# A table of places for every step, turns written as an integer, and eight centrings moved to TensorE, in a kernel of two transformer layers

## The reference, cut to what matters

```python
xn = _layernorm(x)                         # first block
x = x + _L0_attn_ref(xn, ...) + _L0_ffn_ref(xn, Wg, Wu, Wd)
#   _L0_attn_ref: linear attention (elu + 1), layer norm, gated FFN of 341, layer norm
#   _L0_ffn_ref:  sum over 8 experts of silu(x @ Wg) * (x @ Wu) @ Wd, FFN 512, all tokens
xn = _layernorm(x)                         # second block
x = x + _L1_attn_ref(xn, ...) + _L1_ffn_ref(xn, ...)

# _L1_attn_ref, four times over:
x = x + _attention(_layernorm(x, ln1w, ln1b), aw, ab, pw, pb)
h = _layernorm(x, ln2w, ln2b)
x = x + gelu(h @ fw + fb) @ mw + mb
# _attention: q, k, v = h @ aw + ab; each becomes a quaternion
#   [x, x - previous token, x rolled by one head, cos(x)]
# out = hamilton(hamilton(q, k), v) -> spectral filter -> first part -> @ pw + pb
# _L1_ffn_ref: each token goes to the 2 best of 8 experts, gated FFN of 512, weighted sum
```

## Time and profile before

| | |
|---|---|
| median of 3 runs | 1509.45 us (1508.14 to 1509.75) |
| span of the profiled execution | 1503.8 us, first to last instruction |
| what lies around the span, against the median | 5.6 us |
| PE busy | 1395.6 us, 93% |
| DVE busy | 1250.3 us, 83% |
| ACT busy | 1042.7 us, 69% |
| POOL busy | 360.9 us, 24% |
| mean TensorE clock granted | 0.981 of full |

### The profile page before, as it was taken

How to read it: one execution, slowest core, us unless ns; L and a number is a source line. 1 busy time by engine, 2 the same in 40 slices (tenths; PEclk the granted TensorE clock), 3 DMA queues, 4 the chain that set the end, 5 groups by cost and what they waited for, 6 DMA issues and landing times.

```text
span 1503.8 us, 20880 instructions
## 1 busy us (share of the span) xinstructions
PE 1395.6 (93%) x6198; PEld 990.6 (66%) x6198; DVE 1250.3 (83%) x1511; ACT 1042.7 (69%) x2411; POOL 360.9 (24%) x251
## 2 busy tenths in 40 slices
PE   6999999999899999899999899999889999999858
PEld 4677766666566666566665667656677677777636
DVE  3344467877999989999959897999999999999996
ACT  6455757676886777766877768777857787776652
POOL 0001203110221402011131411131543353344410
PEclk9999999999999999999999999999999999999989
DMA  7763445335544554533363335355555556555244
GB/s 270 261 255 139 157 146 185 118 114 168 167 135 148 179 164 135 206 117 111 109 216 113 99 107 168 121 155 174 162 184 167 158 176 198 162 174 160 86 112 155
DMA packets 111243, 238.02 MB, mean 158 GB/s; under 512 B 13207, under 2 KB 52844, under 8 KB 109644
## 3 DMA queue, kind: packets, MB, share of 16 engines
q1 hardware_dynamic: 106588, 227.31, 47.9%
q0 software_dynamic: 4544, 9.38, 1.8%
HBM read 185.59 MB, written 43.86 MB: 153 GB/s over the span
## 4 chain that ended last, share of the span: by engine, by line
PE 44%; issue 20%; DVE 16%; ACT 9%; POOL 8%; DMA 2%; SPq 0%; ACTq 0%; POOLq 0%; DVEq 0%
PE bank L1363 8%; PE bank L1351 7%; PE bank L1353 6%; PE bank L1352 6%; POOL RSTD L1025 4%; PE bank L1543 3%; DVE AM L1087 3%; POOL ytok L1040 3%; ACT ROWS L865 2%; PE bank L1458 2%; DVE SH L1217 2%; DVE TA L1083 2%; PE bank L1452 1%; ACT ROWS L878 1%; DVE TA L1092 1%
## 5 line engine op out<-in xcount | busy, mean ns | idle before, releaser
L1025 POOL TENSOR_TENSOR RSTD<-SS,power_half 128x4 f32<-128x4 f32 x96 | 158.8, 1654 | 816.7 <-ACT ROWS L865 816.5
L1363 PE MATMUL bank<-SH,WD 128*128 128x512 f32 x512 | 263.6, 596 | 0.8 <-DVE X L1233 0.8
L1351 PE MATMUL bank<-NH,GU 128*128 128x512 f32 x512 | 245.5, 479 | 2.0 <-DMA GU<-halves 1.0
L1217 DVE TENSOR_TENSOR SH<-SH,bank 128x512 f32<-128x512 f32 x256 | 172.4, 682 | 76.4 <-ACT SH L853 46.4
L1087 DVE TENSOR_TENSOR AM<-AM,TA 128x1024 f32<-128x1024 f32 x192 | 230.2, 1219 | 0.9
L1083 DVE TENSOR_TENSOR TA<-QKV 128x2048 f32<-128x2048 f32 x96 | 219.5, 2287 | 1.2
L1353 PE MATMUL bank<-NL,GU 128*128 128x512 f32 x512 | 203.0, 397 | 0.0
L1352 PE MATMUL bank<-NH,GU 128*128 128x512 f32 x512 | 202.6, 396 | 0.0
L853 ACT ACTIVATE SH<-bank 128x512 f32<-128x512 f32 x256 | 153.1, 605 | 59.6 <-PE bank L1353 57.5
L878 ACT ACTIVATE ROWS<-bank,RSTD 128x128 f32<-128x128 f32 x384 | 110.0, 374 | 56.2 <-POOL RSTD L1025 50.8
L1578 PE MATMUL bank<-XT,GU 128*128 128x256 f32 x624 | 147.5, 381 | 0.3 <-DVE SH L1335 0.3
(11 more groups left out here) (232 smaller groups left out, 2764.8 us busy)
## 6 DMA issues: line engine op xcount, KB each, us to landing
GU<-halves SPq DMA_DIRECT2D x112, 512.0 KB, 4.2
QKV<-QKV SPq DMA_DIRECT2D x32, 720.0 KB
GU<-in_w_gu SPq DMA_DIRECT2D x39, 512.0 KB, 3.6
xg<-in_c_fill SPq DMA_DIRECT2D x8, 2080.0 KB
WD<-in_w_d SPq DMA_DIRECT2D x128, 128.0 KB, 2.2
FC<-ready_w SPq DMA_DIRECT2D x32, 512.0 KB, 5.2
WQ<-ready_w SPq DMA_DIRECT2D x32, 384.0 KB, 4.8
WD<-in_w_d SPq DMA_DIRECT2D x39, 256.0 KB, 3.8
```

The costliest lines, as they stand in the source:

```text
L1025: pool.tensor_tensor(RSTD[:], SS[:], (power_one if k[0] == "at" else power_half)[:], ALU.pow).then_inc(power_done, 1)
L1217: dve.tensor_tensor(SH[:, g % 4, :], SH[:, g % 4, :], banks[2 + g % 2][:], ALU.mult).then_inc(h_ready, 1)
L1351: pe.matmul(out, w_hi, x_hi, start=True, stop=False)
L1363: pe.matmul(banks[4][:], WD1[:, slot, :], SH[:, g % 4, :], start=first, stop=last).then_inc(down_done, 1)
```

## The change

Three things are changed.

First, the turns of q, k and v are written once, as an integer: `turns` (ACT) writes x / 2 pi + 1/4 into an int32 view of `TURNS`, which rounds it; `reduce` (DVE) multiplies that integer by 2 pi and subtracts x; `cosines` takes Sin with a bias of plus or minus half pi. The step `round`, one ACT instruction of 1536 columns for each of the 32 layers, is gone. `turns` now waits for the earlier `cosines`, since it writes the buffer that these read.

Second, in four layers, (7, 3), (7, 2), (6, 3) and (5, 3), both scalings (A and C) are centred by PE, as in the first block: 8 scalings lose their DVE step, and ACT squares with a constant bias.

Third, the planner and its numbers are gone. `PLACES` has for each step and engine the place in that engine's list; `schedule()` only turns it into lists. As sets, the lists hold the same steps as before but for the 32 `round` and the 8 `centre` on DVE. No step of PE stands more than 13 of 969 places away from where it stood, none of DVE more than 25 of 1217.

```diff
-TURN = 6.283185
-class Plan:
...
+TURN = 2 * np.pi
+HALF_PI = 1.570796
+INSIDE = 1 - 2.5e-7
+CENTRED_BY_PE = ((7, 3), (7, 2), (6, 3), (5, 3))
+PLACES = {
+    "raw": {
+        "SP": (0, 1, 5, 8, 15, 21, 27, 30,),
+    },
...
+TAKES_PART = {
+    ("centre", "DVE"): lambda key: key[0] in ("A", "C") and key[1:3] not in CENTRED_BY_PE,
...
-    token_means = [x for x in scalings if x[0] in ("A", "C")]
+    token_means = [x for x in scalings if x[0] in ("A", "C") and x[1:3] not in CENTRED_BY_PE]
...
-    sums_before = count_before("ACT", ("keys_exp", "query"), lambda name, key: name == "scale" and key[0] == "at")
+    sums_before = count_before("DVE", ("keys_exp", "query"), lambda name, key: name == "normed" and key[0] == "at")
...
             elif name == "turns":
                 h = half_of[k]
                 act.wait_ge(view_read, upto("views", k + (2,)))
-                act.activation(own(QKV[:, h, :, 3, :]), own(QKV[:, h, :, 0, :]), ACT.Identity, bias=quarter[:],
+                act.wait_ge(cos_done, n)
+                act.activation(TURNS[:].bitcast(I32), own(QKV[:, h, :, 0, :]), ACT.Identity, bias=quarter[:],
                                scale=1.0 / (2 * np.pi)).then_inc(turns_done, 1)
-            elif name == "round":
-                h = half_of[k]
-                act.wait_ge(turns_done, upto("turns", k))
-                act.wait_ge(cos_done, n)
-                act.activation(TURNS[:], own(QKV[:, h, :, 3, :]), ACT.Identity, bias=rounder[:]).then_inc(rounded, 1)
             elif name == "cosines":
                 h = half_of[k]
                 act.wait_ge(reduced, upto("reduce", k))
-                act.activation(own(QKV[:, h, 0:2, 3, :]), TURNS[:, 0:2, :], ACT.Sin, scale=-TURN)
-                act.activation(own(QKV[:, h, 2, 3, :]), TURNS[:, 2, :], ACT.Sin, scale=TURN).then_inc(cos_done, 1)
+                act.activation(own(QKV[:, h, 0:2, 3, :]), TURNS[:, 0:2, :], ACT.Sin, bias=half_pi[:], scale=-INSIDE)
+                act.activation(own(QKV[:, h, 2, 3, :]), TURNS[:, 2, :], ACT.Sin, bias=minus_half_pi[:], scale=INSIDE).then_inc(cos_done, 1)
...
             elif name == "reduce":
                 h = half_of[k]
-                dve.wait_ge(rounded, upto("round", k))
-                dve.scalar_tensor_tensor(TURNS[:], TURNS[:], ROUND, own(QKV[:, h, :, 3, :]),
-                                         ALU.subtract, ALU.subtract).then_inc(reduced, 1)
+                dve.wait_ge(turns_done, upto("turns", k))
+                dve.scalar_tensor_tensor(TURNS[:], TURNS[:].bitcast(I32), TURN, own(QKV[:, h, :, 0, :]),
+                                         ALU.mult, ALU.subtract).then_inc(reduced, 1)
```

More of the change, by code:

```diff
@@ L10 @@
 BF16 = mybir.dt.bfloat16
+I32 = mybir.dt.int32
 ALU = mybir.AluOpType
@@ new lines, with step_keys @@
+TAKES_PART = {
+    ("centre", "DVE"): lambda key: key[0] in ("A", "C") and key[1:3] not in CENTRED_BY_PE,
+    ("centre", "ACT"): lambda key: key[0] != "at",
+    ("normed", "ACT"): lambda key: key[0] in ("n0", "n1", "n3", "A", "C"),
+    ("normed", "DVE"): lambda key: key[0] != "n3",
+    ("route", "ACT"): lambda key: key[1] in (0, 2),
+    ("route", "PE"): lambda key: key[1] == 2,
+    ("route", "DVE"): lambda key: key[1] != 2,
+}
+def step_keys():
+    lt = [(t, l) for t in range(TILES) for l in range(LAYERS)]
+    scalings = [(kind, t) for kind in ("n0", "at", "n1", "n2", "n3") for t in range(TILES)]
+    scalings += [(kind, t, l) for kind in ("A", "C") for t, l in lt]
+    tiles, blocks = list(range(TILES)), list(range(BLOCKS))
+    twice = [(g, i) for g in blocks for i in range(2)]
+    out = {name: list(range(n)) for name, n in (
+        ("raw", EXPERTS), ("split", EXPERTS), ("keep", EXPERTS), ("visit", TILES * SPAN // 2), ("split_attn", 1),
+        ("load_prep", LAYERS), ("prep", LAYERS), ("prep_centre", LAYERS), ("keep_prep", LAYERS), ("load_gain", 1),
+        ("last_down", 1), ("kv_sum", BATCHES), ("load_numbers", 1), ("table", 2))}
+    for name in ("fill", "add_experts", "keys", "keys_exp", "query", "ffn2_down", "ffn2_add", "save", "logits", "load_kept",
+                 "total", "load_y", "back", "merge", "out"):
+        out[name] = tiles
+    for name in ("load_w", "load_x", "turn_in", "down", "y_out"):
+        out[name] = blocks
+    for name in ("gate_up", "silu", "mult", "y_store"):
+        out[name] = twice
+    for name in ("load_q", "load_f", "load_p", "load_m", "roll", "turns", "differences", "reduce", "cosines", "fold", "freq",
+                 "gain", "proj", "proj_add", "fc_a", "fc_b", "mproj", "mlp_add"):
+        out[name] = lt
+    for name in ("centre", "power", "scale", "turn", "normed"):
+        out[name] = scalings
+    out["den"] = [(t,) for t in tiles]
+    out["expert"] = [(t, s) for t in tiles for s in range(SPAN)]
+    out["ffn2"] = [(t, c) for t in tiles for c in range(3)]
+    out["route"] = [(t, i) for t in tiles for i in range(4)]
+    out["scatter"] = [(t, i) for t in tiles for i in range(2 * GROUPS)]
+    out["views"] = [(t, l, j) for t, l in lt for j in range(VIEWS)]
+    out["ham"] = [(t, l, i) for t, l in lt for i in range(HAM + 2)]
+    return out
@@ L1050, in _ @@
         dve.memset(every_row[:], 1.0)
[L1051 removed]
+        dve.memset(half_pi[:], HALF_PI)
+        dve.memset(minus_half_pi[:], -HALF_PI)
         dve.memset(quarter[:], 0.25).then_inc(const_set, 1)
```

658 lines of the change are left out of this document (354 added, 304 removed), and 129 rows, old and new, of the table PLACES.

## The result

| | before | after |
|---|---|---|
| median | 1508.9 us (1508.14 to 1509.75, 4 runs) | 1483.97 us (1483.49 to 1484.69, 4 runs) |
| span of the profiled execution | 1503.8 us | 1482.2 us |
| mean clock granted | 0.981 | 0.990 |

The ratio is 0.9835, 95% interval 0.9821 to 0.9849. The forecast of 1485.4 us is 1.4 us off, and the range 1465 to 1503 holds the time. The sum behind it was less good than that: its total was near, its parts were not where it put them.

A forecast was written before the change was run, and what follows sets the result against it. PE was taken to lead from 200 to 1000 us and DVE from 1000 to 1477; 8.8 in the first, 6.1 + 9 in the second and 0.1 at the end make 24.0 us, 1509.45 to 1485.4 us, range 1465 to 1503.

The forecast's parts named there:

- The median against the span: Whole run: the sum was made against the 1503.8 us span, with the median kept 5.6 us above it.
- First stretch, 8.8 us: 200 to 1000 us, where PE leads: half of PE's 17.6 us of named waits saved by the new places; bounds 0 and 41.6.
- the very same neighbours: First stretch: four PE gaps (about 327, 503, 793, 850 us) whose neighbouring steps are unchanged, against five with more work ahead.
- SP and POOL: I count nothing: Weight loads and fills: they keep their distance to their users by a few steps, so 0 us was counted.
- Second stretch, 6.1 + 9 us: 1000 to 1477 us, where DVE leads: 6.1 us from seven centre steps off DVE, 9 us of its 21.2 us idle.
- The latency of a scaling: `turn` of layer (5, 3): some 3 us off PE's 5.13 us gap, 1.4 us of it seen by DVE.
- beside the other engines: ACT: 32 `round` steps, 51.5 us, leave an engine with slack; counted only through waits, not by itself.
- The integer operand: 32 `reduce` steps on DVE: reading int32 costs zero; the rival that it costs gave 1515 us, chance 0.07 with all else slower.
- the end: After the last `freq`, layer (7, 3): PE's queue decides and the new order gives 0.1 us.
- the counts: Signs in the profile: `round` absent, DVE's row sums 56 instead of 64, ACT busy near 994 us.
- The lists are not a new plan: All lists: each `freq` stands behind nearly the same expert work as before, with shifts of a few steps.

The follow-up runs named there:

- new_swap: Changed kernel with one DVE row sum back behind the first product of layer (4, 0) and `fill` 7 back ahead of its roll: 1490.8 us, 0.9891 of the kernel before.
- old_fill: Kernel before with one SP instruction moved, `fill` 7 behind the rolls of (4, 0) and (3, 2): 1503.9 us, 0.9979 of the kernel before.
- new_ctr2: Changed kernel with the eight centre steps back on DVE, three of them placed earlier than in a first try: 1490.4 us, 0.9885 of the kernel before.
- old_ctr: Kernel before, its own lists, with only the eight scalings centred by PE and their DVE steps dropped: 1508.9 us, 1.0005 of the kernel before.

## Why the prediction was right, and where it was not

- **The median against the span: 3.8 us, by luck on my side.** I carried 5.6 us between span and median. Each later profiled execution has a time of its own, and it is 1.8 us over its span in all of them (1484.02 for 1482.2 after). So the span that I worked from belonged to an execution some 3.8 us quicker than the median that I set it against, if the same holds for it. Against the span the forecast was 24.0 us and the gain 21.6; against the median it was 24.9. The sum was 2.4 us too hopeful (1479.8 against a span of 1482.2) and the distance 3.8 us too long, and what is left of the two is the 1.4 us.
- **First stretch, 8.8 us: too small, and for another reason.** It gave 14.5 us, and 15.9 if counted from the first `freq` behind 200 us, where the changed kernel was 1.4 us late. Half of 17.6 us of waits, 14.5 of them at `turn`, was to go; those at `turn` fell by 0.7 us only. For the same work, from that `freq` to the end of the first block's experts, PE's idle time fell by 7.7 us (40.5 to 32.8) and its busy time by 8.2 (748.0 to 739.8, at a clock of 0.99 and 1.00). So the size of the saved idle time was near and its place wrong, and the sum had no term for the clock in this stretch. Two thirds of the 14.5 us came from the part with the two stalls. Both, at 793 and 850 us, I had listed among the places with "the very same neighbours": I looked at PE's list alone, and the cause of the first stood in DVE's and SP's.
- **"SP and POOL: I count nothing": failed.** new_swap and old_fill show that `fill` 7 and one DVE step set 3 to 8 us. I had asked only who uses what the fill writes, and not which transfer was queued behind it: the roll behind it took 9.0 us instead of 5.1.
- **Second stretch, 6.1 + 9 us: too large, it gave 7.0 us** to the last `freq`. The 6.1 us of centring are real in the lists that were made for them (at most 7.1 us, new_ctr2) and nil in the old ones (old_ctr). Most of the 9 us from DVE's idle time did not come: DVE's wait for Silu fell by 4.1 us, that for XSH rose by 4.5. For the same work, from the end of the first block's experts to the last `freq` (447.4 us before, 440.5 after), DVE's busy time fell by 4.1 us (426.7 to 422.6) and its idle time by 2.8 (20.7 to 17.9). From 1000 us to 1455, just ahead of the last `freq`, DVE is busy 437.08 of 455 us, the 96% that I expected, so it does lead; it led before too.
- **The latency of a scaling.** At layer (5, 3) the gap at `turn` went from 5.13 to 1.91 us, as expected; the `turn` of (4, 3) has none. But a gap of 4.06 us stands at the `turn` of scaling A of layer (7, 3), at 1412.78 us, and a low stretch of the clock stands there now (0.86 from 1405 to 1430 us). Over the eight scalings the way from `centre` to `turn` is only 2.4 us shorter than before (55.8 to 53.4 us): at C of (5, 3) it became 3.4 us shorter, at C of (6, 3) 4.8 us longer. The rule of the Trainium skill that I weighed against this term, page "SBUF — State Buffer", section Terms (a shared port pair taken as a lock), from which I took it that a square that ends earlier may only wait longer, is borne out in part: POOL's step at scaling C of (5, 3) again ended 0.87 us after a DVE product with two SBUF inputs, as the rows below show, but in the same lists the shorter scaling kept 0.8 of its 0.87 us (new_ctr2). DVE and POOL after, at scaling C of layer (5, 3), to be held against the earlier trace rows:

```profile
1419.70 2.29 DVE L1302 TENSOR_TENSOR TA<-AM,QKV 128x2048 f32<-128x2048 f32 x1
...
1421.45 1.41 POOL L1234 TENSOR_TENSOR RSTD<-SS,power_half 128x4 f32<-128x4 f32 x1 [9.91 <-ACT ROWS L1078]
```

- **`round` "beside the other engines": right for the old lists, wrong for these.** Its removal alone is worth 0.2% there and 2.6% here. I had put its effect into the waits, with no price of its own.
- **The integer operand, the end, the counts: right.** 1752 ns, 0.1 us, 56 sums. ACT's busy time is 1003.7 us where I expected 994; 5.9 us of the difference are Sin's (32 times 91 and 93 ns), which now has a bias tile; the other 3.8 stay open. The Trainium skill, page "ScalarE: Activation LUTs", section What ACT_TABLE_LOAD costs, gives about 93 ns for each operand that is a pointer to a column; the two groups agree with it, and I could have had this term before the run.
- **"The lists are not a new plan": misleading.** They are near the old ones in place, at most 13 places on PE, and yet 1.75% worse with the old work and 1.4% better than the old ones with the new. My sum added the terms of work and of lists as if each could be had alone. They can't: the work alone is 4 us, the lists alone are -26 us, both are 25.

What stays open: how much of the 39 us a good place for `round` would save; where in the second half of the table the rest of its gain arises; and what sets the low clock near 850 us. The two places that new_swap puts back explain 10.0 of the 14.5 us of the first stretch by the traces, some 8 by the runs.

## What to carry to other kernels

In a kernel whose engines go through fixed lists, a step's price is what stands behind it in its list when its input is late, not its share of a busy engine: the same ACT pass cost 0.2% in one order and 2.6% in another. Read every long stall back through all engines, the DMA queue too, and look at the granted clock around it before counting waits by kind. And when an order is tuned to its work, test order and work apart and together, and put a removed step back at more than one place before calling its cost its own. And a stall and a low clock side by side are not yet cause and effect: near 850 us a low clock stood here with the stall next to it and without it.
